# Index tiles in a ring of eight, and a gather queue that waits for products itself

## The chip, the cores and the metric
One core of a Trainium2 chip. The metric is the device time of one launch in microseconds; the kernel before takes 5577.5 us (median of 3 runs, 5574.76 to 5580.09). Lower is better.

## What is computed
One graph layer with 12,500 nodes of 128 features and 412,500 edges, sorted by destination.

```
f      = x @ W1            (node features; a second part, self, stays with the node)
w      = gelu(gelu(edge_attr_8 @ W_mlp1) @ W_mlp2) @ Wp     (radial weights of each edge)
mid    = products of w, f[src] and edge_attr_4              (per edge; scalars and vectors mixed)
n      = segment_sum(mid, dst)                              (over the edges of each node)
out    = layernorm(x + cos * self + sin * (n @ W2))
```

All of it is float32. The order of edges and the indices are data: f[src] is a gather from a table in DRAM.

## The kernel before
**Start.** The node features are computed (PE), copied (DVE) and stored as `feature_table` in DRAM; source indices are transposed to `src_all` (int16, one column for each tile of 128 edges). `acc` holds the 12,500 nodes' sums in SBUF.

**Main loop.** Edges are worked on in 202 blocks of 2048, each 16 tiles of 128 edges, or 4 chunks of 4 tiles. Each engine has its own list of instructions, a loop of 25 rounds of 8 steps (POOL: of 4 steps), and they meet only in semaphores. For block b:

- ACT copies 16 index columns from `src_all` to `idx` as int32 (`copy_indices`, L496) and increments `s_idx`.
- POOL waits for `s_idx`, and issues 16 indirect DMAs (`gather`, L429), each of which brings 128 rows of 512 bytes from the table to `gath`, a ring of 4 slots. They increment `s_g[slot][chunk]` on landing.
- PE makes the radial weights: two layers for block b+4 (L700, L705; their gelus are ACT L512 and L517) and the weights of block b by chunks into four PSUM banks (L715, `s_w[c]`).
- DVE multiplies weights and gathered rows (`products`, L957 and L960, `s_prod[c]`), when `s_w[c]`, `s_g[slot][c]` and `s_seg[c]` of the block before are there.
- PE sums the products into windows of 8 nodes (L729, `s_seg[c]`); ACT copies the sums (L531), PE transposes them (L740), ACT copies that (L538, L539), PE multiplies by W2 (L748, `s_y`), and DVE adds 16 windows to `acc` (L985).
- SP loads edge attributes (L341) and, for two blocks at a time, edge_attr_8 (L337).

The order on each engine is written out by hand in its function `step`. On DVE it is: product chunks 0 and 1, `select` for the next block, chunk 2, loading of 16 window addresses, chunk 3, the additions of block b-1. On PE: radial 0, sums 2 of b-1, first layer, radial 1, sums 3 of b-1, second layer, radial 2, transposes of b-1, sums 0, first layer, radial 3, sums 1, the product with W2 of b-1, second layer, transposes of b.

**What frees a slot.** ACT does it for POOL. At the head of step b, ACT waits until DVE has done chunk 3 of block b-1, and then copies the indices of block b+3, whose slot in `gath` and in `idx` is that of b-1. POOL itself waits for nothing but `s_idx`:

```
act.wait_ge(s_prod[CHUNKS - 1], b + 0)
copy_indices(b + (SLOTS - 1), (s + SLOTS - 1) % SLOTS).then_inc(s_idx, 1)
```

A second branch (`Else`) of every engine is for graphs in which the nodes of a group of edges spread over more than 8; it isn't taken with these inputs. After the loop the nodes are normalised and stored.

Of the kernel before, what the change touches and what calls it, by code (L numbers as in the profile page):

```python
# [43 lines left out]
SLOTS = 4  # L44
# [21 lines left out]
def build_program(nc, x, src, dst, ea4, ea8, W1_0e, W1_1o, W_mlp1, W_mlp2, Wp, W2_0e, W2_1o, out):  # L66
# [3 lines left out]
    with ctx:  # L70
        def sb(name, shape, dt=FP32):
            return ctx.enter_context(nc.sbuf_tensor(name, shape, dt))
# [9 lines left out]
        big = sb("big", [128, NODE_TILES * FEAT])  # L82
        dst_rows = sb("dst_rows", [128, ROWS, 256])
        rel_all = sb("rel_all", [128, ALL_GROUPS * 2], BF16)
        src_all = sb("src_all", [128, (BLOCKS + 2) * TILES], INT16)
        gath = sb("gath", [128, SLOTS, TILES, FEAT])
        idx = sb("idx", [128, SLOTS, TILES], INT32)
        ea_t = sb("ea_t", [128, RING, TILES, 4])
        ea_last = sb("ea_last", [128, TILES, 4])
        e8 = sb("e8", [128, RING, 128])  # L90
# [197 lines left out]
        def _(sp):  # L288
# [71 lines left out]
            with sp.If(flag < WINDOW):  # L360
# [16 lines left out]
                for i in range(PAIRS):  # L377
                    sp.wait_ge(s_tr, 2 * ROUNDS + (i // 2 - 1))
                    for r in range(2 * i, 2 * i + 2):
                        load_e8(r, min((b + r) * BLOCK, LAST_START))  # L380
            with sp.Else():
                with sp.Fori(1, BLOCKS - 1) as b:
                    sp.wait_ge(s_gblk, b + 1)
                    load_e8(0, b * BLOCK)
                    sp.dma_start(ea_t[:, 0, :, :], ea4[bass.ds(b * BLOCK, BLOCK), :].rearrange("(t q) k -> q t k", q=128))\
                        .then_inc(s_ea[0], 16)
                sp.wait_ge(s_gblk, BLOCKS)
                load_e8(0, LAST_START)
# [8 lines left out]
        @block.gpsimd  # L397
        def _(pool):
            pool.memset(wfeat[:, :], 0.0).then_inc(s_zero_node, 1)
            pool.memset(wself_raw[:, :], 0.0).then_inc(s_zero_node, 1)  # L400
            pool.memset(ident[:, :], 0.0).then_inc(s_ident0, 1)
            pool.wait_ge(s_ident0, 1)
            pool.affine_select(out=ident[:, :], in_=ident[:, :], compare_op=ALU.not_equal, fill=1.0, base=0,
                               pattern=[[-1, 128]], channel_multiplier=1).then_inc(s_ident, 1)
            pool.memset(dst_rows[:, ROWS - 1, :], 0.0).then_inc(s_rows, 1)
            pool.iota(iota_i[:, :], pattern=[[1, WINDOW]], base=0, channel_multiplier=0).then_inc(s_iota, 1)
            pool.memset(eps_col[:, :], EPS).then_inc(s_iota, 1)
            pool.memset(w1bd[:, :, :], 0.0).then_inc(s_zero, 1)
            pool.memset(w2bd[:, :], 0.0).then_inc(s_zero, 1)
            pool.memset(wpbd[:, :], 0.0).then_inc(s_zero, 1)  # L410
            pool.memset(conv_stage[:, :, :], 0.0).then_inc(s_zero, 1)
            pool.memset(ea_last[:, :, :], 0.0).then_inc(s_eal0, 1)
            pool.wait_ge(s_zero, 4)
            for to, of in loop_weights[:POOL_WEIGHT_LOADS]:
                pool.dma_start(to, of).then_inc(s_wts_pool, 16)

            for c in range(ROWS):
                pool.wait_ge(s_min, c + 1)
                for e in range(2):
                    half = slice(128 * e, 128 * (e + 1))  # L420
                    last = pool.tensor_scalar(dst_rows[:, c, half], dst_rows.bitcast(INT32)[:, c, half],
                                              base_f[:, ROWS * e + c:ROWS * e + c + 1], None, ALU.subtract)
                last.then_inc(s_rel, 1)
            pool.wait_ge(s_xts, -(-(SRC_FROM + 2 * ROWS) // BATCH))
            pool.memset(src_rows[:, ROWS - 1, :], 0.0).then_inc(s_srcz, 1)

            def gather(s, c):
                for t in range(CT * c, CT * (c + 1)):
                    pool.indirect_dma_start(out=gath[:, s, t, :], out_offset=None, in_=table[:, :],  # L429
                                            in_offset=bass.IndirectOffsetOnAxis(ap=idx[:, s, t:t + 1], axis=0))\  # L430
                        .then_inc(s_g[s][c], 16)

            def table_stored():
                for i in range(PIECE_SLOTS):
                    pool.wait_ge(s_tab[i], 16 * (len(range(i, PIECES, PIECE_SLOTS)) + (i == (PIECES - 1) % PIECE_SLOTS)))

            table_stored()
            pool.wait_ge(s_flag, 1)
            flag = pool.value_load(flag_i[0:1, 0:1], min_val=0, max_val=NODES)
            with pool.If(flag < WINDOW):  # L440
                for b in range(SLOTS):
                    pool.wait_ge(s_idx, b + 1)
                    for c in range(CHUNKS):
                        gather(b, c)
                with pool.Fori(1, QUADS) as n:
                    for s in range(SLOTS):

                        pool.wait_ge(s_idx, n * SLOTS + (s + 1))
                        pool.sem_inc(s_round, 1)
                        for c in range(CHUNKS):  # L450
                            gather(s, c)
                for b in (BLOCKS - 2, BLOCKS - 1):
                    pool.wait_ge(s_idx, b + 1)
                    for c in range(CHUNKS):

                        if b < BLOCKS - 1 or c >= CUT_C:
                            gather(b % SLOTS, c)
            with pool.Else():
                with pool.Fori(0, BLOCKS) as b:
                    pool.wait_ge(s_idx, b + 1)  # L460
                    pool.sem_inc(s_round, 1)
                    for c in range(CHUNKS):
                        gather(0, c)
# [5 lines left out]
        def _(act):  # L469
# [69 lines left out]
                act.copy(to[:, :, 1:4, :], by_tile(1)[:, :, 1:4, :]).then_inc(s_zt, 1)  # L539

            def step(b, s, k, d_round, first=False, last=False):
                if not last and not first:
                    act.wait_ge(s_prod[CHUNKS - 1], b + 0)
                    copy_indices(b + (SLOTS - 1), (s + SLOTS - 1) % SLOTS).then_inc(s_idx, 1)
                if not first:
                    copy_transposed(b - 1, 0)
                if not last:
                    if s % SUPER == 0:
                        copy_e8T(k)
                    gelu1(b + SUPER, 0)  # L550
                if not first:
                    copy_sums(b - 1, 1)
                if not last:
                    gelu2(b + SUPER, s + SUPER, 0)
                    lay_attributes(b + 1, (s + 1) % RING, d_round * 16 + 16, b + 1, None if first else b + 0)
                if not first:
                    copy_transposed(b - 1, 1)
                if not last:
                    gelu1(b + SUPER, 1)
                copy_sums(b, 0)  # L560
                if not last:
                    gelu2(b + SUPER, s + SUPER, 1)
# [2 lines left out]
            flag = act.value_load(flag_i[0:1, 0:1], min_val=0, max_val=NODES)  # L565
            act.wait_ge(s_rts[0], 2)
            with act.If(flag < WINDOW):
                for b in range(SLOTS):
                    copy_indices(b, b).then_inc(s_idx, 1)
                copy_odd_indices()  # L570
                copy_e8T(0)
# [526 lines left out]
```

## Time and profile before

| | |
|---|---|
| device time, median of 3 | 5577.5 us |
| profiled execution: time, span | 5586.11 us, 5584.3 us |
| busy: PE, PE weight loads | 58%, 32% of the span |
| busy: POOL, DVE, ACT | 56%, 34%, 21% |
| DMA engines, mean | 46 GB/s |
| PE's granted clock, mean | 0.74 of 2.4 GHz |

The profile is of one execution. A group of instructions has a source line, an engine, an operation, and what it writes and reads. Busy time of PE comes from modelled ends of its instructions. "Idle before" is the time in which the engine did nothing ahead of an instruction, with the line that ended this; "remote" or "another core or an unknown queue" stands for a semaphore's update that was not matched with the end of an instruction, and "issue" for no wait that the profile shows. Times in the timeline count from the start of the span.

### The profile page before, as it was taken

What the parts mean: (1) busy time and instruction counts of PE and PEld (TensorE: products, weight loads), DVE (VectorE), ACT (ScalarE), POOL (GpSimd) and SP (SyncE); (2) the same over time, 40 slices, a digit from 0 to 9 for tenths busy, and PEclk for the clock granted to TensorE, in tenths of its full rate; (3) what the DMA queues carried; (4) which work ended last, traced back from release to release, by engine and by line L of the source; (5) the groups of instructions that cost most, each with busy time, mean ns of one, the idle gap of its engine ahead of it and who ended that gap; (6) DMA issues with size and microseconds to landing.
All of it is one profiled execution on the core that took longest, in us unless ns stands there. A gap on an engine that the chain in (4) does not pass through costs nothing.

```text
span 5584.3 us, 54049 instructions
## 1 busy us (share of the span) xinstructions
PE 3213.1 (58%) x15272; PEld 1784.0 (32%) x15272; DVE 1871.9 (34%) x6401; ACT 1200.0 (21%) x2642; POOL 3103.5 (56%) x3281
## 2 busy tenths in 40 slices
PE   5655555555555555555555555555555555556556
PEld 4232333333323333333233333332332333333334
DVE  2233333333333333333333333333333333333335
ACT  2121222112212222222122222221221222222224
POOL 5255555555555555555555555555555556555551
PEclk7677777777777777777777777777777777777777
DMA  6022122221221221222212212122122122221211
GB/s 148 16 45 45 42 43 43 44 44 42 44 46 41 44 45 43 43 43 44 45 41 44 45 43 42 43 44 44 41 44 45 42 43 45 44 43 42 45 45 58
DMA packets 586056, 256.02 MB, mean 46 GB/s; under 512 B 528384, under 2 KB 531868, under 8 KB 584348
## 3 DMA queue, kind: packets, MB, share of 16 engines
q0 software_dynamic: 103616, 211.52, 15.0%
q1 hardware_dynamic: 480572, 42.82, 6.6%
q14 instruction: 160, 1.30, 0.1%
q10 hardware_dynamic: 1696, 0.18, 0.0%
q8 instruction: 12, 0.20, 0.0%
HBM read 241.45 MB, written 12.81 MB: 46 GB/s over the span
## 4 chain that ended last, share of the span: by engine, by line
another core or an unknown queue 50%; PE 31%; issue 10%; ACT 8%; DVE 0%; ACTq 0%; DMA 0%; DVEq 0%; SPq 0%; POOL 0%; POOLq 0%
PE bank L715 9%; PE bank L705 7%; PE bank L700 5%; PE bank L729 4%; PE bank L740 4%; ACT h L512 2%; ACT zsb L531 2%; ACT bank L527 1%; PE bank L657 1%; ACT ztsb L539 1%; ACT ztsb L538 1%; PE bank L696 1%; PE bank L748 1%; ACT big L615 1%
## 5 line engine op out<-in xcount | busy, mean ns | idle before, releaser
L429 POOL DMA_INDIRECT gath<-feature_table,idx x3224 | 3077.3, 955 | 2351.9 <-ACT idx L496 1395.0
L705 PE MATMUL bank<-h,w2bd 128*128 128x512 f32 x820 | 631.2, 861 | 897.3 <-ACT h L512 512.2
L957 DVE TENSOR_TENSOR big<-bank,gath 128x256 f32<-128x256 f32 x808 | 341.8, 423 | 2358.2 <-remote 2112.0
L715 PE MATMUL bank<-wpbd,big 128*128 128x256 f32 x3232 | 986.3, 434 | 50.2 <-issue 49.0
L715 PEld LDWEIGHTS bank<-wpbd,big 128*128 128x128 f32 x3232 | 700.0, 224 | 443.1 <-issue 377.9
L960 DVE TENSOR_TENSOR big<-bank,gath 128x384 f32<-128x384 f32 x1616 | 818.0, 548 | 0.0
L985 DVE TENSOR_TENSOR acc<-acc,bank 128x8 f32 x3232 | 528.5, 164 | 777.5 <-remote 361.2
L748 PE MATMUL bank<-ztsb,conv 128*128 128x128 f32 x1616 | 316.0, 356 | 681.8 <-issue 549.2
L740 PE MATMUL bank<-ident,zsb 128*128 128x128 f32 x1616 | 337.3, 347 | 559.4 <-ACT zsb L531 491.4
L512 ACT ACTIVATE h<-bank 128x512 f32<-128x512 f32 x410 | 244.9, 597 | 1748.9 <-remote 1182.8
L729 PE MATMUL bank<-big,sel 128*32 128x256 f32 x6464 | 560.7, 421 | 9.4 <-DVE big L960 6.8
L700 PE MATMUL bank<-e8T,w1bd 128*128 128x512 f32 x820 | 506.6, 702 | 56.2 <-ACT big L517 38.7
L517 ACT ACTIVATE big<-bank 128x512 f32<-128x512 f32 x410 | 453.2, 1105 | 388.5 <-PE bank L705 254.8
L740 PEld LDWEIGHTS bank<-ident,zsb 128*128 128x128 f32 x1616 | 257.3, 180 | 840.1 <-ACT zsb L531 626.4
L748 PEld LDWEIGHTS bank<-ztsb,conv 128*128 128x128 f32 x1616 | 268.2, 251 | 773.5 <-issue 647.4
L705 PEld LDWEIGHTS bank<-h,w2bd 128*128 128x128 f32 x820 | 158.6, 241 | 1035.9 <-ACT h L512 553.0
L531 ACT COPY zsb<-bank 128x512 f32<-128x512 f32 x404 | 236.1, 584 | 926.0 <-remote 736.5
L538 ACT COPY ztsb<-bank 128x64 f32<-128x64 f32 x404 | 86.9, 215 | 1032.6 <-remote 843.9
L700 PEld LDWEIGHTS bank<-e8T,w1bd 128*128 128x128 f32 x820 | 136.1, 209 | 276.2 <-issue 173.1
L729 PEld LDWEIGHTS bank<-big,sel 128*32 128x32 f32 x6464 | 133.0, 112 | 274.0 <-issue 273.8
L944 DVE TENSOR_TENSOR sel<-rel_all,bank 128x128 f32<-128x128 f32 (+1 forms) x202 | 58.0, 287 | 421.9 <-issue 269.8
L949 DVE TENSOR_TENSOR sel<-sel,bank 128x512 f32<-128x512 f32 x202 | 138.7, 687 | 6.9
(77 smaller groups left out, 794.3 us busy)
## 6 DMA issues: line engine op xcount, KB each, us to landing
gath<-feature_table,idx POOLq DMA_INDIRECT x3224
e<-in_edge_attr SPq DMA_DIRECT2D x416, 32.0 KB
ea_t<-in_edge_attr SPq DMA_DIRECT2D x100, 64.0 KB
feature_table<-gath SPq DMA_DIRECT2D x4, 1280.0 KB, 5.6
out<-big SPq DMA_DIRECT2D x4, 1280.0 KB
big<-in_x SPq DMA_DIRECT2D x3, 1280.0 KB, 8.4
dst_rows<-in_dst SPq DMA_DIRECT2D x1, 1536.0 KB
big<-in_src SPq DMA_DIRECT2D x1, 1408.0 KB
```

The costliest lines, as they stand in the source:

```text
L429: pool.indirect_dma_start(out=gath[:, s, t, :], out_offset=None, in_=table[:, :], in_offset=bass.IndirectOffsetOnAxis(ap=idx[:, s, t:t + 1 ...
L512: act.activation(h1[:, h, :], hid_ps[:, :], ACT.Gelu_apprx_tanh, scale=1.0 / math.sqrt(RADIAL)).then_inc(s_h1[h], 1)
L517: act.activation(h2[:, m // SUPER % 2, :, :, 2 * (m % SUPER) + h], hid_ps[:, :].rearrange("q (b p) -> q b p", b=SUPER), ACT.Gelu_apprx_tan ...
L531: act.copy(zsb[:, :, :], z_ps).then_inc(s_zc, 1)
L700: pe.matmul(hid_ps[:, :], w1bd[:, 2 * (m % SUPER) + h, :], e8T[:, :], start=True, stop=True)\
L705: pe.matmul(hid_ps[:, :], w2bd[:, :], h1[:, h, :], start=True, stop=True).then_inc(s_h2p[h], 1)
L715: last = pe.matmul(wgt_ps[c][:, 256 * r:256 * (r + 1)], h2[:, s // SUPER % 2, s % SUPER, 16 * g:16 * (g + 1), :].rearrange("q p a -> q (p ...
L729: last = pe.matmul(z_ps[32 * t:32 * (t + 1), c % 2, :], sel[:, s % 2, CT * c + t, :, :].rearrange("q k w -> q (k w)"), prod[:, c, t, :], s ...
L740: last = pe.transpose(zt_ps[:, h, c, :], zsb[:, c, 128 * h:128 * (h + 1)], ident[:, :])
L748: last = pe.matmul(y_ps, conv[:, k, :], ztsb[:, k, :], start=(k == 0), stop=(k == 3))
L960: last = dve.tensor_tensor(o[:, :, h, 1:4, :], w[:, :, h, 1, :].unsqueeze(2).to_broadcast([128, n, 3, MUL]), f[:, :, 1:4, :], ALU.mult)
L985: dve.tensor_tensor(acc[:, at], acc[:, at], y_ps[:, WINDOW * t:WINDOW * (t + 1)], ALU.add)\
```

## The change
`idx` becomes a ring of 8 tiles. ACT copies the indices of block b+7 instead of b+3, in the middle of step b instead of at its head, and eight blocks instead of four before the loop. POOL waits for `s_idx` as before, and now also, ahead of each chunk of four gathers, for `s_prod[c]` of the block four back; its loop has 25 rounds of 8 blocks instead of 50 of 4. `s_round` is incremented once for each chunk instead of once for each block. The waits in SP's `Else` are in the branch that isn't taken.

```diff
-        src_all = sb("src_all", [128, (BLOCKS + 2) * TILES], INT16)
+        src_all = sb("src_all", [128, (BLOCKS + RING - 2) * TILES], INT16)
...
-        idx = sb("idx", [128, SLOTS, TILES], INT32)
+        idx = sb("idx", [128, RING, TILES], INT32)
...
             with sp.Else():
+                for i in range(1, PAIRS):
+                    sp.wait_ge(s_e8[i], 64)
+                    sp.wait_ge(s_ea[i], 16)
...
             def gather(s, c):
                 for t in range(CT * c, CT * (c + 1)):
-                    pool.indirect_dma_start(out=gath[:, s, t, :], ...
+                    pool.indirect_dma_start(out=gath[:, s % SLOTS, t, :], ...
...
-                        .then_inc(s_g[s][c], 16)
+                        .then_inc(s_g[s % SLOTS][c], 16)
...
-                for b in range(SLOTS):
+                def gather_block(b, s, free, chunks=range(CHUNKS)):
                     pool.wait_ge(s_idx, b + 1)
-                    for c in range(CHUNKS):
-                        gather(b, c)
-                with pool.Fori(1, QUADS) as n:
-                    for s in range(SLOTS):
-
-                        pool.wait_ge(s_idx, n * SLOTS + (s + 1))
-                        pool.sem_inc(s_round, 1)
-                        for c in range(CHUNKS):
-                            gather(s, c)
+                    for c in chunks:
+                        if free is not None:
+                            pool.wait_ge(s_prod[c], free)
+                            pool.sem_inc(s_round, 1)
+                        gather(s, c)
+
+                for b in range(RING):
+                    gather_block(b, b, b - SLOTS + 1 if b >= SLOTS else None)
+                with pool.Fori(1, ROUNDS) as n:
+                    for s in range(RING):
+                        gather_block(n * RING + s, s, n * RING + (s - SLOTS + 1))
+                gather_block(BLOCKS - 2, 0, BLOCKS - 2 - SLOTS + 1)
+                gather_block(BLOCKS - 1, 1, BLOCKS - 1 - SLOTS + 1, range(CUT_C, CHUNKS))
...
             def step(b, s, k, d_round, first=False, last=False):
-                if not last and not first:
-                    act.wait_ge(s_prod[CHUNKS - 1], b + 0)
-                    copy_indices(b + (SLOTS - 1), (s + SLOTS - 1) % SLOTS).then_inc(s_idx, 1)
...
                 if not first:
                     copy_sums(b - 1, 1)
+                if not last and not first:
+                    act.wait_ge(s_prod[CHUNKS - 1], b + 0)
+                    copy_indices(b + (RING - 1), (s + RING - 1) % RING).then_inc(s_idx, 1)
...
-                for b in range(SLOTS):
+                for b in range(RING):
                     copy_indices(b, b).then_inc(s_idx, 1)
```

## Rows read from the trace of the kernel before

**Rows 1.** The page's chain of work that ended last, by engine.
```profile
another core or an unknown queue 50%; PE 31%; issue 10%; ACT 8%; DVE 0%; ACTq 0%; DMA 0%; DVEq 0%; SPq 0%; POOL 0%; POOLq 0%
```
**Rows 2.** Waits: line, released by, us in total, times, longest us.
```profile
POOL gath L429 <- ACT idx L496: 1395.0, 197, 97.3
...
DVE big L957 <- remote: 2112.0, 266, 15.0
...
ACT h L512 <- remote: 1182.8, 182, 15.0
```
**Rows 3.** The tile idx: duration ns min/median/max, first and last start.
```profile
L429 POOL DMA_INDIRECT gath<-feature_table,idx x3224: 949/955/1071, 70.8 to 5484.6; - x190
L496 ACT CAST idx<-src_all x204: 198/231/245, 68.2 to 5502.3; 128x16 int32 x100, 128x16 int32<-128x16 int16 x2
```
**Rows 4.** Timeline 2055 to 2081: start, duration, what, [idle before <-releaser].
```profile
2055.86 0.95 POOL L429 DMA_INDIRECT gath<-feature_table,idx  x1 [8.09 <-ACT idx L496]
...
2060.19 0.58 ACT L531 COPY zsb<-bank 128x512 f32<-128x512 f32 x1 [0.86 <-PE bank L729]
...
2062.98 1.12 PE L700 MATMUL bank<-e8T,w1bd 128*128 128x512 f32 x2
...
2063.94 1.03 PE L715 MATMUL bank<-wpbd,big 128*128 128x256 f32 x4
...
2074.22 0.60 ACT L512 ACTIVATE h<-bank 128x512 f32<-128x512 f32 x1 [8.06 <-remote]
...
2074.74 0.95 POOL L429 DMA_INDIRECT gath<-feature_table,idx  x1 [0.30 <-issue]
...
2077.05 0.42 DVE L957 TENSOR_TENSOR big<-bank,gath 128x256 f32<-128x256 f32 x1 [12.19 <-remote]
2077.39 1.01 DVE L960 TENSOR_TENSOR big<-bank,gath 128x384 f32<-128x384 f32 x2
...
2078.71 4.59 DVE L985 TENSOR_TENSOR acc<-acc,bank 128x8 f32 x16 [0.31 <-remote]
...
2079.89 0.24 ACT L496 CAST idx<-src_all 128x16 int32 x1
...
2080.92 0.95 POOL L429 DMA_INDIRECT gath<-feature_table,idx  x1 [5.22 <-ACT idx L496]
```
**Rows 5.** Timeline 2038 to 2055, the block before.
```profile
2038.52 1.03 PE L715 MATMUL bank<-wpbd,big 128*128 128x256 f32 x4
...
2039.20 9.74 SPq L337 DMA_DIRECT2D e<-in_edge_attr  x4
...
2046.82 0.95 POOL L429 DMA_INDIRECT gath<-feature_table,idx  x1 [0.30 <-issue]
...
2051.20 0.60 ACT L512 ACTIVATE h<-bank 128x512 f32<-128x512 f32 x1 [4.12 <-remote]
2051.26 0.43 DVE L957 TENSOR_TENSOR big<-bank,gath 128x256 f32<-128x256 f32 x1 [11.22 <-remote]
...
2051.69 0.58 ACT L531 COPY zsb<-bank 128x512 f32<-128x512 f32 x1
...
2054.84 0.23 ACT L496 CAST idx<-src_all 128x16 int32 x1
```
**Rows 6.** Timeline 5490 to 5503, behind the last gather.
```profile
5490.54 0.23 ACT L496 CAST idx<-src_all 128x16 int32 x1
...
5502.26 0.22 ACT L496 CAST idx<-src_all 128x16 int32 x1
```
**Rows 7.** Groups of the page: busy us, mean ns of one, idle before.
```profile
L729 PE MATMUL bank<-big,sel 128*32 128x256 f32 x6464 | 560.7, 421 | 9.4 <-DVE big L960 6.8 <-issue 2.6
L985 DVE TENSOR_TENSOR acc<-acc,bank 128x8 f32 x3232 | 528.5, 164 | 777.5 <-remote 361.2 <-DVE acc L985 16.4 <-PE bank L748 9.2
```
**Rows 8.** Windows 248 to 5512: us, busy (x instructions) of PE, PEld, DVE, ACT, POOL, clock, DMA, GB/s.
```profile
248.00:5512.00 5264.00, 3029.38 (x14575) 1664.33 (x14574) 1765.92 (x5981) 1103.82 (x2446) 3015.95 (x3160) 0.74 0.21 43
```

More of the change, by code:

```diff
@@ L428, in gather @@
                 for t in range(CT * c, CT * (c + 1)):
-                    pool.indirect_dma_start(out=gath[:, s, t, :], out_offset=None, in_=table[:, :],
+                    pool.indirect_dma_start(out=gath[:, s % SLOTS, t, :], out_offset=None, in_=table[:, :],
                                             in_offset=bass.IndirectOffsetOnAxis(ap=idx[:, s, t:t + 1], axis=0))\
-                        .then_inc(s_g[s][c], 16)
+                        .then_inc(s_g[s % SLOTS][c], 16)
             def table_stored():
@@ L440, in _ @@
             with pool.If(flag < WINDOW):
-                for b in range(SLOTS):
+                def gather_block(b, s, free, chunks=range(CHUNKS)):
                     pool.wait_ge(s_idx, b + 1)
-                    for c in range(CHUNKS):
-                        gather(b, c)
-                with pool.Fori(1, QUADS) as n:
-                    for s in range(SLOTS):
-                        pool.wait_ge(s_idx, n * SLOTS + (s + 1))
-                        pool.sem_inc(s_round, 1)
-                        for c in range(CHUNKS):
-                            gather(s, c)
[L452 to L457, printed above, removed]
+                    for c in chunks:
[10 more added lines that the diff above has]
+                gather_block(BLOCKS - 1, 1, BLOCKS - 1 - SLOTS + 1, range(CUT_C, CHUNKS))
             with pool.Else():
```

## The prediction
> **What bounds the kernel now.** I read the chain of waits first: half of the span is put down to "another core or an unknown queue" [rows 1]. With one core there is no other, so this is a release whose source the profile does not match. The waits name it: DVE's product L957 waits 2112.0 us for "remote" and ACT's L512 1182.8 us, while POOL waits for ACT's index copy 197 times [rows 2]. Without the longest wait (97.3 us, the start) that is (1395.0 - 97.3) / 196 = 6.62 us for each block.
>
> Then the timeline. POOL's 16 gathers of a block start 1.26 us apart, from 2055.86 to 2074.74, and end at 2075.69: a run of 19.83 us, 5.03 us for each chunk of four. The next run starts at 2080.92, right behind the index copy at 2079.89 [rows 4]. Run plus mean pause: 19.83 + 6.62 = 26.45 us a block. All the rest of a step, when no gather is under way, takes far less: the last two index copies, after the last gather (5484.6 [rows 3]), are 5502.26 - 5490.54 = 11.7 us apart [rows 6]. So neither PE's work (3029.38 us busy in 5264 us, 15.2 us a block [rows 8]) nor POOL's alone sets 26.45 us; something ties them.
>
> Rows 4 show what. PE's first-layer matmul starts at 2062.98 and its radial matmuls at 2063.94, but their consumers start at 2074.22 (ACT L512, 8.06 us "remote") and 2077.05 (DVE L957, 12.19 us "remote"). Early in the same run nothing is late: at 2060.19 ACT follows PE by its own 0.86 us. So some 5.5 us into a run of gathers PE's results begin to reach the others late. Between ACT L512 and DVE L957 lie four recorded matmuls: 2.83 / 4 = 0.71 us each, however small. When the run ends, everything comes at once [rows 5]: POOL's last gather ends at 2047.77 and ACT L512, DVE L957 and ACT L531 start at 2051.20, 2051.26 and 2051.69, on results of three different PE groups. I call this the release: 2078.71 - 2075.69 = 3.0 us behind the end of a run, 3.5 us in rows 5, where SP's e8 loads (L337, 9.74 us) lie in the run.
>
> The loop is therefore a circle: gathers run, PE's results stall, gathers end, release, ACT finishes the step, ACT copies indices, gathers run. Each block holds one run and one pause.
>
> The Trainium skill (Perfetto Trace Analysis, Summary: the profiler window per engine type) says that a TensorE record's end is only estimated, and what follows it is hidden. By it PE could really be executing that slowly; the common release in rows 5 speaks for late delivery, and the forecast is the same by both, since it uses only when consumers start.
>
> **The change, part by part.**
> *Index ring of eight, seven ahead.* In a step the index copy moves from the head to behind copy_sums. It stays one copy of 0.24 us [rows 4] on ACT, so a step's total keeps it; where it stands now it can delay gelu2 by 0.24 us, where it stood it delayed the transposed copy as much. I take 0. Four more copies in the prologue are 4 x 0.24 = 1 us at most, hidden by POOL's 97.3 us wait. The waits in SP's other branch are not executed. What the move does is to take ACT, and PE's last layer behind which ACT stands, out of POOL's circle: the copy for a block is done seven steps before.
>
> *POOL's waits.* Each chunk now waits for products(b-4, c). POOL may run up to four blocks ahead instead of starting block b+3 at step b. Could it run on for ever? No: a block has 14575 / (5264 / 26.45) = 73 recorded matmuls [rows 8], and at 0.71 us each PE would pass 52 us a block while POOL gathers one in 20. So POOL runs out of free chunks, pauses, and the release follows. What changes is what a pause consists of and how often it comes. Behind the waiting instruction stand only POOL's own gathers. They are needed four blocks later, so nobody else waits for them.
>
> *Length of a pause.* Before: release, rest of the step on ACT (gelu, last layer, gelu), index copy, POOL's start: 6.62 us in the mean; 8.1 us between rows 5 and rows 4 (in front of 2055.86) and 5.2 us at the end of rows 4. After: release (3.0 us without, 3.5 us with e8 loads), the product that frees the chunk (2077.05 to 2078.40, 1.35 us), POOL's start (index copy's end 2080.13 to gather 2080.92, 0.8 us): 5.15 to 5.65 us, mean 5.4.
>
> *How often.* A run now ends where the products are four blocks back, not after 16 gathers. From a release, PE goes on undisturbed through the pause and about 5.5 us of the next run: 2.2 + 5.5 = 7.7 us of an 11.7 us step. Then 12 us and more of the run at 0.71 us a matmul pass some 20 of 73, and at the next release what PE has done meanwhile comes at once (rows 5: the layer, the radial chunk, the sums: 8 records for a chunk's sums alone [rows 7], some 20). That is 0.66 + 0.27 + 0.27 = 1.2 blocks for each run, or 4.8 chunks. I take 4.5 chunks, half way between this and the present 4, since the e8 loads slow half of the runs: 4 / 4.5 = 0.9 pauses a block.
>
> *A pause on chunk 0.* If POOL stops in front of chunk 0, the product it needs stands behind DVE's 16 window additions (4.59 us from 2078.71; 164 ns each [rows 7]), which themselves wait for the release: 3.0 + 4.6 + 1.35 + 0.8 = 9.8 us. I take one pause in eight as such: 0.9 x (9.8 - 5.4) / 8 = 0.5 us a block.
>
> *Cost of the added waits.* Four waits with a register and four increments a block where there was one. No row shows a satisfied wait between two chunks. Lower bound 0: they lie under the 0.95 us of the gather before. Upper bound: each costs POOL's 0.8 us start anew, 3 more = 2.4 us. I take 0.3 us, near the lower, because address arithmetic between chunks is already hidden there (all starts 1.26 us apart).
>
> *Sum.* Pause time a block: 0.9 x 5.4 + 0.5 + 0.3 = 5.7 us against 6.62: 0.9 us less. Over 196 blocks: 176 us. The profiled execution took 5586.11 us (span 5584.3), 8.6 us over the median of the three runs: 5586 - 176 = 5410, less 9: 5400 us.
> Ends: 5 chunks a run, short release, no cost of waits: 0.8 x 5.15 = 4.1 us, so 2.5 x 196 = 490 us less, 5087. Waits at their upper bound: 2.1 x 196 = 412 us more than the forecast, 5810.
>
> **Rivals.**
> *A, POOL stops at chunk 0 (slower).* If the weights of chunk 3 become visible before POOL has done its four chunks, POOL takes that chunk too and stops in front of chunk 0, where the pause is 9.8 us. With five chunks a run: 0.8 x 9.8 + 0.3 = 8.1 us a block, 1.5 us more than now, 297 us: 5875 us. It decides at 15 to 17 us after a run's start. For it: a chunk-0 stop leaves DVE and PE far advanced, so it may repeat itself. Against it: in rows 4 chunk 3's weights come at 2077.05, 21 us after the run's start, and in rows 5 only with the release.
> *B, nothing gained.* One pause a block remains, and the 1.2 us that it gets shorter are lost to slower results, since each run begins earlier in PE's step and more of the step falls into it: 26.45 us a block, 5577 us.
> *C, gathers free of interference (much faster).* If what delays PE's results is the burst after a wait and not gathering itself, steps take 11.7 us and POOL's 20.1 us a block bounds: 5577 - 6.3 x 196 = 4340 us. The Trainium skill (SBUF — State Buffer, SBUF: two separate sides) says that DMA ports and engine ports cannot contend and that PE never waits for anyone's port; by that rule PE should be as fast beside gathers as without, and the time would be rival C's. The trace does not agree: 12.19 us late beside them [rows 4], 11.7 us for a whole step without [rows 6].
>
> **How the numbers follow.** Forecast 0.58, rival A 0.24, B 0.12, C 0.06. A change under 0.2% (11 us) is not told from none. Faster: 0.58 + 0.06 and a quarter of B: 0.67. Same: half of B, 0.06. Slower: 0.24 and the rest of B: 0.27. The forecast's own range is 5087 to 5570. The range goes from 5060 to 5830: it leaves out C and the worse half of A.
>
> **What would show it.** POOL L429 then waits for DVE L960, not for ACT L496. Right: pauses of 5 to 6 us, fewer than one a block, POOL's idle time before L429 down by some 180 us; DVE L957 still "remote". Wrong: most pauses near 10 us in front of chunk 0, behind L985 (A); more than one pause a block, or gathers more than 1.26 us apart at chunk borders (the waits' price); "remote" gone (C). If DVE waited for a gather itself, the claim that gathers are early enough would be wrong.

## The result, and the profile after

The changed kernel takes 5652.75 us (median of 4 runs, 5633.84 to 5687.63) against 5578.8 us for the kernel before on the same chip (4 runs, 5574.76 to 5584.6). The ratio is 1.0139 (95% interval 1.0087 to 1.019): 1.4% slower. The forecast was 5400 us, so the direction was wrong; the range of 5060 to 5830 holds the time. On other chips, reached by the experiments, the same change makes the kernel 0.24% faster; that comes last among them.

The profiled execution took 5646.39 us with a span of 5644.4 us, 60.1 us more than before. First the page: two groups and the shares of the chain of waits.

```profile
L432 POOL DMA_INDIRECT gath<-feature_table,idx x3224 | 3077.2, 954 | 2407.5 <-issue 1719.1
...
L986 DVE TENSOR_TENSOR acc<-acc,bank 128x8 f32 x3232 | 528.1, 163 | 1574.9 <-remote 1137.2
...
another core or an unknown queue 44%; PE 32%; issue 15%; ACT 6%; DVE 2%; DVEq 0%; DMA 0%; ACTq 0%; SPq 0%; POOL 0%; POOLq 0%
```

The 3224 gathers are as busy as before, and the idle time ahead of them is 2407.5 us, where it was 2351.9 us: 55.6 of the 60.1 us stand there. The line of the window additions (now L986) waits 1137.2 us for late results, where it was 361.2 us [rows 7]. The waits name who releases POOL, and what DVE and ACT wait for (line, released by, us in total, times, longest).

```profile
POOL gath L432 <- issue: 1719.1, 3033, 83.2
...
DVE big L958 <- remote: 1287.9, 194, 14.9
DVE acc L986 <- remote: 1137.2, 145, 18.3
...
ACT h L513 <- remote: 745.6, 94, 20.0
...
POOL gath L432 <- DVE big L961: 688.4, 191, 10.4
```

ACT's index copy no longer releases POOL; DVE's product L961 does, as predicted. The view names it for 112 of the 213 pauses counted below and says "issue" for the other 101 (a good part of the semaphores' updates isn't in this trace, see under Open); but in 212 of the 213 POOL starts 0.77 to 0.79 us after the end of an L961. "Remote" has not gone. It has moved: 2112.0 us at the products and 1182.8 us at ACT's first gelu before [rows 2], now spread over the products, the additions and ACT. The usual 0.30 us between gathers (the median) stayed at chunk borders too, so a satisfied wait costs nothing to see.

I then went through all gathers of the trace from block 5 on and took every gap over 1.2 us as a pause:

| kernel | pauses | mean us | sum us | chunks per run | where |
|---|---|---|---|---|---|
| before | 197 | 6.60 | 1300.9 | 4.0 | chunk 0 always |
| after | 213 | 6.41 | 1364.4 | 3.7 | chunk 0: 162, mean 6.87; chunk 1: 27, 5.10; chunk 2: 4, 8.21; chunk 3: 19, 4.21; one within a chunk |

Pauses cost 63.5 us more, the start 14 us less (the pause ahead of block 4, 97.25 before, is 83.22 us), and the other gaps 6 us more: 55.6 us.

Three pauses in four are in front of chunk 0. One of the long ones in full, from the timeline (start, duration, what, idle before):

```profile
1872.24 0.95 POOL L432 DMA_INDIRECT gath<-feature_table,idx  x1 [0.30 <-issue]
1875.22 0.58 ACT L532 COPY zsb<-bank 128x512 f32<-128x512 f32 x1 [11.58 <-remote]
...
1876.04 1.10 ACT L518 ACTIVATE big<-bank 128x512 f32<-128x512 f32 x1 [0.23 <-remote]
1876.10 4.59 DVE L986 TENSOR_TENSOR acc<-acc,bank 128x8 f32 x16 [8.61 <-remote]
...
1880.66 0.42 DVE L958 TENSOR_TENSOR big<-bank,gath 128x256 f32<-128x256 f32 x1
1881.00 1.01 DVE L961 TENSOR_TENSOR big<-bank,gath 128x384 f32<-128x384 f32 x2
...
1882.80 0.95 POOL L432 DMA_INDIRECT gath<-feature_table,idx  x1 [9.60 <-DVE big L961]
```

The run's last gather ends at 1873.19. DVE's additions begin 2.91 us later, on the release; the product of chunk 0 can only follow them at 1880.66, ends at 1882.01, and POOL starts 0.79 us after. 2.9 + 4.6 + 1.35 + 0.8 = 9.6 us: this is rival A's pause, term for term.

Not every pause on chunk 0 is like it. Two blocks earlier the additions fell into the run itself:

```profile
1817.44 4.61 DVE L986 TENSOR_TENSOR acc<-acc,bank 128x8 f32 x16 [4.16 <-remote]
...
1822.62 0.95 POOL L432 DMA_INDIRECT gath<-feature_table,idx  x1 [0.30 <-issue]
1825.82 0.42 DVE L958 TENSOR_TENSOR big<-bank,gath 128x256 f32<-128x256 f32 x1 [3.78 <-remote]
...
1826.16 1.01 DVE L961 TENSOR_TENSOR big<-bank,gath 128x384 f32<-128x384 f32 x2
...
1827.94 0.95 POOL L432 DMA_INDIRECT gath<-feature_table,idx  x1 [4.36 <-issue]
```

I sorted the 213 pauses by whether all 16 additions stand between the run's end and the product that ends the pause. 64 hold them: 10.14 us in the mean, 648.9 us in sum, all on chunk 0. The other 149 have a mean of 4.80 us, 715.5 us in sum.

### The profile page after: what moved, and what is told of

It reads as the page before. It is cut to its first block, busy times and chain, and to the rows that moved or that the text cites. A ratio compares the mean times of both kernels' runs of the same rounds, so it can differ in the third digit from the quotient of the medians.

```text
span 5644.4 us, 54565 instructions
## 1 busy us (share of the span) xinstructions
PE 3152.4 (56%) x15272; PEld 1726.7 (31%) x15272; DVE 1866.7 (33%) x6401; ACT 1227.9 (22%) x2646; POOL 3103.4 (55%) x3281
## 3 DMA queue, kind: packets, MB, share of 16 engines
q0 software_dynamic: 103616, 211.52, 14.4%
## 4 chain that ended last, share of the span: by engine, by line
another core or an unknown queue 44%; PE 32%; issue 15%; ACT 6%; DVE 2%; DVEq 0%; DMA 0%; ACTq 0%; SPq 0%; POOL 0%; POOLq 0%
PE bank L716 9%; PE bank L701 7%; PE bank L706 5%; PE bank L730 5%; PE bank L741 2%; ACT h L513 2%; ACT zsb L532 1%; ACT big L518 1%; PE bank L749 1%; PE bank L658 1%; DVE acc L986 1%; ACT ztsb L540 1%; DVE big L961 1%; ACT big L616 1%
## 5 line engine op out<-in xcount | busy, mean ns | idle before, releaser
L432 POOL DMA_INDIRECT gath<-feature_table,idx x3224 | 3077.2, 954 | 2407.5 <-issue 1719.1
L716 PE MATMUL bank<-wpbd,big 128*128 128x256 f32 x3232 | 1063.2, 462 | 250.9 <-issue 249.7
L986 DVE TENSOR_TENSOR acc<-acc,bank 128x8 f32 x3232 | 528.1, 163 | 1574.9 <-remote 1137.2
L716 PEld LDWEIGHTS bank<-wpbd,big 128*128 128x128 f32 x3232 | 751.5, 239 | 731.3 <-issue 654.9
L701 PE MATMUL bank<-e8T,w1bd 128*128 128x512 f32 x820 | 585.3, 803 | 662.7 <-ACT big L518 258.7
L706 PE MATMUL bank<-h,w2bd 128*128 128x512 f32 x820 | 524.6, 726 | 691.1 <-ACT h L513 396.3
L961 DVE TENSOR_TENSOR big<-bank,gath 128x384 f32<-128x384 f32 x1616 | 816.6, 546 | 0.0
L741 PE MATMUL bank<-ident,zsb 128*128 128x128 f32 x1616 | 301.5, 318 | 737.9 <-issue 402.4
L730 PE MATMUL bank<-big,sel 128*32 128x256 f32 x6464 | 587.8, 440 | 23.0 <-DVE big L961 22.8
L741 PEld LDWEIGHTS bank<-ident,zsb 128*128 128x128 f32 x1616 | 229.9, 164 | 918.1 <-issue 525.6
L706 PEld LDWEIGHTS bank<-h,w2bd 128*128 128x128 f32 x820 | 143.4, 219 | 818.3 <-ACT h L513 437.3
L749 PE MATMUL bank<-ztsb,conv 128*128 128x128 f32 x1616 | 235.4, 289 | 9.9 <-issue 9.9
L749 PEld LDWEIGHTS bank<-ztsb,conv 128*128 128x128 f32 x1616 | 196.9, 192 | 93.4 <-issue 93.4
```

The costliest lines, as they stand in the source:

```text
L432: pool.indirect_dma_start(out=gath[:, s % SLOTS, t, :], out_offset=None, in_=table[:, :], in_offset=bass.IndirectOffsetOnAxis(ap=idx[:, s, ...
L701: pe.matmul(hid_ps[:, :], w1bd[:, 2 * (m % SUPER) + h, :], e8T[:, :], start=True, stop=True)\
L706: pe.matmul(hid_ps[:, :], w2bd[:, :], h1[:, h, :], start=True, stop=True).then_inc(s_h2p[h], 1)
L716: last = pe.matmul(wgt_ps[c][:, 256 * r:256 * (r + 1)], h2[:, s // SUPER % 2, s % SUPER, 16 * g:16 * (g + 1), :].rearrange("q p a -> q (p ...
L730: last = pe.matmul(z_ps[32 * t:32 * (t + 1), c % 2, :], sel[:, s % 2, CT * c + t, :, :].rearrange("q k w -> q (k w)"), prod[:, c, t, :], s ...
L741: last = pe.transpose(zt_ps[:, h, c, :], zsb[:, c, 128 * h:128 * (h + 1)], ident[:, :])
```

## The experiments

Each is told against the kernel before on its own chip, since that takes 5677.96 us on the chip of e1 to e4 (5667.03 to 5687.19), 5583.56 on that of e5 to e8 (5581.25 to 5594.34), and 4216 to 4217 on the three of e9 to e18. Pauses are counted as above. All edits are to the changed kernel unless said otherwise.

### e1: one wait a block, for chunk 3

```diff
+                    if free is not None:
+                        pool.wait_ge(s_prod[CHUNKS - 1], free)
+                        pool.sem_inc(s_round, 1)
                     for c in chunks:
-                        if free is not None:
-                            pool.wait_ge(s_prod[c], free)
-                            pool.sem_inc(s_round, 1)
                         gather(s, c)
```

> The changed kernel with one wait of POOL a block in place of four: before the first gather of a block it waits for products chunk 3 of the block four back. Theory (the time is 20.1 us of gathers plus a pause whose length is set by the product that POOL waits for): every pause ends behind chunk 3, 3.0 to 3.5 us release + 1.35 us product + 0.8 us start = 5.2 to 5.6 us, 25.5 us a block, about 5400 us; pauses on chunk 0 behind DVE's additions are gone. Rival 1 (PE's late results are a budget of so much a block, wherever the pause lies): one pause of 6.6 us or more a block remains, 5580 to 5650 us. Rival 2 (the four waits and increments a block are what the change costs): 5590 us, as before.

5597.82 us is the median of four runs (5517.66, 5596.82, 5598.83 and the profiled 5611.24 us). The ratio, 0.9814 (0.9739 to 0.9888), is of the three others, and leans on the 5517.66; by the medians it is 0.986. The time is within rival 1's 5580 to 5650 us and above the theory's 5400. The edit asks for the same product as the kernel before does through ACT, so it is the change without its chunk waits: ACT's late end of the step is out of POOL's way. It gains between 1.1 and 2.6% on this chip, but its 197 pauses are not what I had priced: 6.71 us in the mean (1321.8 us in sum), where my term was 5.4. (No trace shows the kernel before on this chip; on the first its pauses were 6.60 us.) A pause of its timeline says why:

```profile
1904.73 0.95 POOL L432 DMA_INDIRECT gath<-feature_table,idx  x1 [0.30 <-issue]
...
1908.66 0.42 DVE L958 TENSOR_TENSOR big<-bank,gath 128x256 f32<-128x256 f32 x1 [1.90 <-remote]
...
1909.00 1.01 DVE L961 TENSOR_TENSOR big<-bank,gath 128x384 f32<-128x384 f32 x2
...
1910.00 0.42 DVE L958 TENSOR_TENSOR big<-bank,gath 128x256 f32<-128x256 f32 x1
...
1910.35 1.01 DVE L961 TENSOR_TENSOR big<-bank,gath 128x384 f32<-128x384 f32 x2
...
1911.42 4.60 DVE L986 TENSOR_TENSOR acc<-acc,bank 128x8 f32 x16
...
1912.13 0.95 POOL L432 DMA_INDIRECT gath<-feature_table,idx  x1 [6.44 <-issue]
```

At the release (1908.66, 3.0 us behind the run's end at 1905.68) DVE has two chunks' products before it, not one: 3.0 + 2 x 1.35 + 0.8 = 6.5 us. So it is in 138 of its 197 pauses; 51 hold one chunk's product. I read this as a run that begins earlier in the step and leaves more of the step to the next release.

### e2: one wait a block, for chunk 0

```diff
+                    if free is not None:
+                        pool.wait_ge(s_prod[0], free + 1)
+                        pool.sem_inc(s_round, 1)
```
The chunk waits are taken out as in e1. All pauses now lie in front of chunk 0, whose product stands behind the additions in DVE's order.

> The same with the wait for products chunk 0 of the block three back, so that every pause ends behind chunk 0 and thus behind the 16 additions. Theory: release 3.0 + additions 4.6 + product 1.35 + start 0.8 = 9.8 us each, at most 29.9 us a block, 6250 us; but PE and DVE are further on when gathers start again, so some releases come before a run's end: 6.9 us, the mean of the changed kernel's pauses on chunk 0, is the lower end, 5650 us. Rival 1 (a budget of late results): the same time as with chunk 3. Rival 2 (cost of waits): faster than the changed kernel by the same as with chunk 3.

6002.12 us (5969.63 to 6015.14), ratio 1.0554 (1.0514 to 1.0594). It lies in the range that was written down, 5650 to 6250 us. 172 pauses of 9.89 us in the mean, some 4.6 chunks to a run. That the mean meets the 9.8 us worked out for a pause on chunk 0 is luck: sorted as above, 104 pauses hold the additions, with a mean of 13.05 us, and 68 don't, with 5.07. It is the slowest kernel of all. Its idle time ahead of the gathers:

```profile
L432 POOL DMA_INDIRECT gath<-feature_table,idx x3224 | 3085.8, 957 | 2762.6 <-issue 2356.7 <-DVE big L961 405.9
```

### e3: the additions moved behind chunk 0 of the next block

In DVE's step, chunk 0 of the next block is multiplied first, and then the additions are made. (The last block gathers all four chunks, 8 gathers more.)

```diff
-                for c in range(CHUNKS):
+                for c in range(1, CHUNKS):
...
+                if not last:
+                    products(b + 1, s + 1, 0, round_ + ((s + 1) % SLOTS == 0))
```

> The changed kernel with DVE's 16 additions of block b-1 moved behind product chunk 0 of block b+1 (POOL's waits as in the change; the last block's first two chunks are gathered too, 10 us of POOL beside other work). Theory: the pauses on chunk 0 lose the 4.6 us of additions; with 157 pauses of 6.85 us there, of which those over 6 us stand behind additions, some 2 to 4 us a block less: 4900 to 5250 us. Rival 1 (budget): within 1% of 5650 us. Rival 2: 5650 us too, since the waits stay.

5476.24 us (5457.23 to 5500.91), ratio 0.9636 (0.961 to 0.9661): 3.6% under the kernel before on that chip. Less than I wrote down (4900 to 5250), but the direction is clear. Pauses on chunk 0 fall to 131 with a mean of 4.70 us; in all there are 240, 3.3 chunks to a run, and their sum is 1148.3 us. One of them:

```profile
1799.60 0.42 DVE L958 TENSOR_TENSOR big<-bank,gath 128x256 f32<-128x256 f32 x1 [11.09 <-remote]
1799.94 1.01 DVE L961 TENSOR_TENSOR big<-bank,gath 128x384 f32<-128x384 f32 x2
...
1800.87 2.81 DVE L986 TENSOR_TENSOR acc<-acc,bank 128x8 f32 x10
...
1801.75 0.95 POOL L432 DMA_INDIRECT gath<-feature_table,idx  x1 [4.71 <-DVE big L961]
```

The product is now first at the release and POOL starts 2.15 us after it. None of the 240 pauses holds the additions in front of its product. Together with the sorting of the changed kernel's pauses (10.14 us with the additions, 4.80 without) and of e2's (13.05 and 5.07) this shows the additions as what makes the long pauses long.

### e4: a quarter of the gathers

`gather` issues one tile of a chunk's four from block 4 on, and the products wait for 16 increments each; the other rows are not fetched.

> The changed kernel with one gather for each chunk instead of four from block 4 on (three of four tiles of gathered rows are stale; it leaves out three quarters of the gathers). Theory (gathers delay PE's results, and what PE has queued comes when they end): POOL's part is 5 us a block, PE's results are hardly ever late, a step takes 12 to 18 us, 2700 to 3900 us. Rival (PE with its throttled clock and the chain over three engines need some 25 us a block anyway): 5300 to 5600 us.

2788.46 us, ratio 0.4912 (0.4901 to 0.4923), within the theory's range, and a view of the main loop by its window (columns as in [rows 8]):

```profile
248.00:2700.00 2452.00, 2366.55 (x14496) 1345.65 (x14493) 1747.24 (x5951) 1112.77 (x2433) 752.13 (x786) 1.00 0.20 29
```

PE is busy 97% of this window at a granted clock of 1.00, the upper level of 2.4 GHz, where it was 58% at 0.74 [rows 8]. So the rival, a throttled PE that needs some 25 us a block anyway, is out. No "remote" of any size is left (79.3 us is the largest, in the preparations). Late results need the dense gathers; whether by their number or by their bytes this run can't tell, since it cuts both. A block takes (2700 - 248) / 196 = some 13 us.

### e5: 24 more matmuls a block (on the kernel before)

```diff
-                pe.matmul(hid_ps[:, :], w1bd[:, 2 * (m % SUPER) + h, :], e8T[:, :], start=True, stop=True)\
+                for q in range(4):
+                    last = pe.matmul(hid_ps[:, 128 * q:128 * (q + 1)], w1bd[:, 2 * (m % SUPER) + h, :],
...
```

The matmuls of both layers, cut from 512 columns into four of 128.

> The kernel before with each of the four 128x512 layer matmuls of a block cut into four of 128x128: the same columns, 24 more recorded matmuls a block (97 for 73). Theory (while gathers run, PE's results pass one recorded matmul in 0.71 us, however small): of the 24 some two thirds fall into the late part of a run, 16 x 0.71 = up to 11 us a block, less what the release takes at once: 2 to 8 us a block, 5950 to 7100 us. Rival (PE computes slowly beside gathers, by columns): the time of the kernel before within 2%.

5823.95 us, ratio 1.0426 (1.0405 to 1.0447); pauses 197 as before, mean 7.76 instead of 6.60. Neither expectation holds: 24 more matmuls added (5823.95 - 5583.56) / 196 = 1.2 us a block, below the 2 to 8 us and above the rival's 2%. This does not refute a fixed time for each late matmul. A run is 16 gathers long in both kernels, so by that account it passes as many late matmuls in both, and what is left over is done after the release. PE's busy time alone grew by about 1 us a block (3029.38 us in 5264 us before, 3187.59 us in 5442 us here). The times of PE's own semaphore updates say more. Where two in a row are late, the time from one to the next over four recorded radial matmuls is 2.86 us (median of 55 pairs) before and 2.85 us (135 pairs) here, again 0.71 us for each; over the eight recorded matmuls of a cut second layer it is 3.59 us (53 pairs), 0.45 us for each. All these scatter widely, and what the rate goes by stays open.

### e6, e7, e8: the same edits on another chip

e6 is e1 and e3 together. e7 is the changed kernel once more. e8 is the kernel before with e3's move of the additions only.

> One wait a block for chunk 3 together with the additions moved behind the next chunk 0. Theory: with one wait on chunk 3 no pause stands behind the additions, so the move brings nothing more than it did alone at chunk 3: ratio 0.97 to 0.985, and no better than the moved additions with four waits (0.964). Rival (the moved additions also let PE's product with W2 and so the rest of a step come earlier): the two gains add up, ratio 0.945 to 0.955.

> The changed kernel itself on the chip of the other runs, for a comparison on one chip. Expected the same ratio to the kernel before as at first, 1.01 to 1.02.

> The kernel before, with nothing changed but the additions of block b-1 moved behind chunk 0 of block b+1 (and the last block's first two chunks gathered too). Theory (the additions count only where a pause of POOL ends behind them; before, it ends behind ACT's index copy): within 1% of the kernel before. Rival (the additions are on the step's path whatever POOL waits for): 3% faster or more, as in the changed kernel.

| | us | ratio to before | pauses | mean us | sum us |
|---|---|---|---|---|---|
| e6 | 5629.32 | 1.009 (1.0062 to 1.0119) | 196 | 6.73 | 1318.5 |
| e7 | 5674.63 | 1.0165 (1.0144 to 1.0186) | 220 | 6.28 | 1382.4 |
| e8 | 5763.87 | 1.0318 (1.0294 to 1.0343) | 197 | 7.48 | 1472.8 |

e7 repeats the result: 162 pauses on chunk 0, mean 6.86, as in the first trace. e6 is 0.9% slower than before on this chip, although both of its parts were faster on theirs; neither its theory (0.97 to 0.985) nor its rival met it. Its pauses are e1's (6.71), and not e3's (4.78): behind one wait for chunk 3 the place of the additions doesn't matter to POOL. It is 0.8% faster than e7, the changed kernel on the same chip (5629.32 to 5674.63 us). e8's expectation, within 1% of before, was wrong: moving the additions is no gain in itself. PE's product with W2 then waits longer for ACT's copy of the transposed sums, in the groups of the kernel before and of e8:

```profile
L748 PE MATMUL bank<-ztsb,conv 128*128 128x128 f32 x1616 | 316.0, 356 | 681.8 <-issue 549.2 <-ACT ztsb L539 132.4
...
L746 PE MATMUL bank<-ztsb,conv 128*128 128x128 f32 x1616 | 325.0, 363 | 948.2 <-ACT ztsb L537 581.6 <-issue 364.4 <-DVE sel L947 2.2
```

The idle time ahead of it grew by 266 us, and it lies in the part of the step whose end ACT's index copy stands behind. That this is what makes e8 slower is my reading; no run tests it. e3's gain isn't that of the move alone: neither with ACT's release (e8) nor with one wait a block (e6) do the pauses get shorter, only with the chunk waits, whose pauses on chunk 0 it cuts.

### e9 to e12: the bytes, and the candidates once more

e9 is the changed kernel with gathers of 32 elements a row instead of 128 from block 4 on (128 instead of 512 bytes; the rest of a row is not fetched, and as the indices stay as they are, the pieces all come from the first quarter of the table). e10 repeats e1, e11 e3, e12 the changed kernel.

> The changed kernel with gathers of 32 elements (128 bytes) a row instead of 128 (512 bytes) from block 4 on: as many gathers and rows, a quarter of the bytes (the products then use rows of which three quarters are stale). If the bytes that the gathers move are what delays PE's results: much nearer to the quarter gathers' 2788 us, 3000 to 4500 us. If it is the number of gathers or of their rows: within 3% of the changed kernel, some 5500 to 5700 us.

> One wait a block, chunk 3 four back, on one chip with the changed kernel. Theory: 1 to 3% faster than the changed kernel (its pauses are 6.7 us, 193 of them, against 6.85 us on chunk 0 plus some 50 shorter ones). Against the kernel before 0.98 to 1.00, since on the chip of the first comparison the kernel before itself took 5678 us and not 5580.

> The changed kernel with the additions moved behind the next chunk 0, once more on one chip with the changed kernel. Theory: 3 to 5% faster than the changed kernel; against the kernel before 0.96 to 0.985.

> The changed kernel on this chip, for the comparison with the two above: 1.01 to 1.02 of the kernel before if that ratio is the same on every chip; 0.99 to 1.00 if the kernel before is slower on this chip and the changed one is not.

The chip of these runs was another. The kernel before takes 4216.99 us there (32 runs, 4215.0 to 4218.5), 24% less than on the first, and the expectations had been made for late results.

| | us | ratio to before |
|---|---|---|
| e9 | 4206.79 | 0.9977 (0.9967 to 0.9988) |
| e10 | 4216.59 | 0.9999 (0.999 to 1.0008) |
| e11 | 4215.88 | 0.9998 (0.9989 to 1.0007) |
| e12 | 4206.57 | 0.9976 (0.9966 to 0.9985) |

The changed kernel's waits on this chip, with the chain of its page:

```profile
DVE big L958 <- DMA gath<-feature_table,idx: 1113.2, 384, 3.9
PE bank L730 <- DVE big L961: 1075.5, 507, 6.5
...
POOL 68%; issue 23%; PE 6%; ACT 1%; DVE 1%; DMA 1%; POOLq 1%; ACTq 0%; DVEq 0%; SPq 0%
```

"Remote" is gone, DVE waits for gathers, and POOL never pauses behind its first wait for a slot: its gaps are 0.30 us, and the longest is 0.60. A block takes 16 x 1.26 = 20.2 us, which is rival C's world (forecast as 4340 us). ACT starts right behind PE in the middle of a run of gathers, in a fourth run of the changed kernel (e16, below):

```profile
2002.05 1.13 PE L701 MATMUL bank<-e8T,w1bd 128*128 128x512 f32 x2
...
2003.21 0.60 ACT L513 ACTIVATE h<-bank 128x512 f32<-128x512 f32 x1 [2.52 <-PE bank L701]
```

PE ends at 2003.18 by the record, ACT starts 0.03 us later; before, the same pair was 10.1 us apart [rows 4]. The number of bytes makes no difference here (e9 beside e12), because POOL takes 955 ns for a gather of either width. Whether fewer bytes would make results less late where they are late stays open.

### e13 to e18: the same, again

e13 to e16 repeat the four on one more chip, e17 and e18 repeat e3 and the changed kernel on another. Both are of the kind without late results (before: 4216.29 and 4216.8 us).

> The changed kernel with rows of 128 bytes from block 4 on (three quarters of each gathered row are stale). Where the kernel before takes some 5600 us: if the bytes of the gathers are what delays PE's results, 4200 to 4900 us; if it is the number of gathers or their rows, within 3% of the changed kernel. Where it takes 4217 us, nothing is told apart: 4207 us again.

> One wait a block for chunk 3. Where the kernel before takes some 5600 us (PE's results late): 1 to 3% faster than the changed kernel on the same chip. Where it takes 4217 us: the same as all.

> The additions behind the next chunk 0, with four waits. Where the kernel before takes some 5600 us: 3 to 5% faster than the changed kernel on the same chip, since the pauses on chunk 0 lose the additions. Rival (the gain of 3.6% at first came from that chip, where the kernel before took 5678 us): no faster than the changed kernel. Where it takes 4217 us: the same as all.

> The changed kernel on the same chip. Where the kernel before takes some 5600 us: 1.01 to 1.02 of it. Where it takes 4217 us: 0.998 of it, since POOL's gathers alone set the time of both.

> The additions behind the next chunk 0, with four waits. Where the kernel before takes some 5600 us: 3 to 5% faster than the changed kernel on the same chip. Rival: no faster than it. Where the kernel before takes 4217 us: the same as all.

> The changed kernel beside it. Where the kernel before takes some 5600 us: 1.01 to 1.02 of it. Where it takes 4217 us: 0.998 of it.

4206.67 (0.9978), 4215.65 (1.0), 4215.11 (0.9998), 4206.46 (0.9976), 4215.1 (0.9995) and 4206.63 us (0.9975), each with an interval of about 0.001 to both sides and as written down for chips of this kind. They settle where the 0.24% comes from. POOL's first wait for a slot, ahead of block 4, in e14 (one wait a block) and then in e16 (the changed kernel):

```profile
168.80 0.96 POOL L432 DMA_INDIRECT gath<-feature_table,idx  x1 [17.70 <-issue]
```
```profile
158.96 0.95 POOL L432 DMA_INDIRECT gath<-feature_table,idx  x1 [8.03 <-issue]
```

By chunks it waits 8.03 us once, by blocks 17.70: the 9.7 us are the whole difference between 4215.65 and 4206.46. e15 starts as early (8.59 us) and gives it back with its 8 more gathers, 8 x 1.26 = 10.1 us. The 14 us that the changed kernel gains at its start on the first chip are the same saving: with late results the pause ahead of block 4 is 83 to 86 us in the four traces with chunk waits (the changed kernel twice, e3, e4) and 94 to 99 us in the six others.

## Why the prediction was wrong

**The circle: right.** Gathers run, results come late, the release follows 2.9 to 3.0 us behind a run's end in the pauses shown, POOL's idle time holds the loss. e4 and e9 to e18 show both sides: without dense gathers, and on chips without late results, nothing of it is left.

**Ring and index copy: right.** ACT's copy is out of POOL's waits, and no row shows a cost of it.

**Cost of the added waits: taken as 0.3 us a block, measured 0.** The median gap is 0.305 us at a chunk border and within a chunk.

**Length of an ordinary pause: right, and somewhat long.** 5.4 us counted the release, one chunk's product and POOL's start. The 149 pauses without the additions have a mean of 4.80 us, since many releases come less than 3.0 us after a run's end (2.25 us in the short one shown). (In e1, with one wait for chunk 3, most pauses hold two products and the mean is 6.71 us; that is rival B's mechanism, but it isn't what the changed kernel does: there 211 of 213 pauses hold one.)

**A pause on chunk 0: the step that failed.** I took one pause in eight as standing behind the additions, 22 of 176. Measured: 162 of 213 pauses are on chunk 0, and 64 of them, three in ten of all, hold the 16 additions. Their price was right (9.8 us forecast, 10.14 us measured). In the sum from block 5 on: forecast 154 x 5.4 + 22 x 9.8 = some 1050 us and 59 us for the waits; measured 715.5 + 648.9 = 1364 us. So the ordinary pauses gave 116 us less than forecast and the waits 59 us less, and the pauses behind the additions cost 433 us more. That is the whole miss.

**How often: also off.** I took 4.5 chunks a run (176 pauses); it is 3.7 (213 pauses). The ordinary pauses number 149 against 154, so the surplus is again the pauses behind the additions.

The two hang together. A run that starts on chunk 0 goes on for four chunks; chunks 1 to 3 are free and chunk 0 isn't, since DVE stands ahead of the additions or in them. 107 of the 207 runs that start between 300 and 5450 us are of exactly 16 gathers. I had called this rival A and gave it 0.24; its place and its mechanism are what happened, and its 5875 us was too high because it put the additions into every pause. Against it I had put that chunk 3's weights come late in a run. That spoke about runs of the kernel before, which begin at another point of the step, and so decided nothing. That the range of 5060 to 5830 us holds the time owes something to luck: its upper end was made of 2.1 us a block for waits that cost nothing.

**A reading of rows 4 that was loose.** The 0.86 us that the prediction gives as ACT's distance behind PE is ACT's idle time ahead of that copy; PE's L729 ended 0.07 us before it. Nothing in the sum uses it.

**What holds in place of "fewer pauses".** In five traces with late results the time lost in pauses hardly depends on how POOL's runs are cut. e1, e6, the changed kernel twice and the kernel before lie between 1301 and 1382 us with 196 to 220 pauses. I read this as PE and DVE needing a certain quiet time for each block, which runs of gathers don't give; moving the stop trades number for length. e2, with the additions in 104 of 172 pauses (1701.9), and e3, with none in the way (1148.3), break out. So do e8 (1472.8) and e5 (1528.5), both with ACT's release as before. That this quiet time is a fixed need was not tested by itself.

**Open.** What makes results late in some runs and not in others. The first comparison and e1 to e8 had them, e9 to e18, on three other chips, did not; but each chip that is named on record was used at one time only, and all the late runs came before all the others, so that chip and time aren't told apart. It isn't that the gathers' own packets take longer: 14.4% of the span is 813 us in the changed kernel on the first chip, and 19.3% is 811 us in e12.

```profile
q0 software_dynamic: 103616, 211.52, 14.4%
...
q0 software_dynamic: 103616, 211.52, 19.3%
```

One thing goes with the lateness in the traces: semaphore updates are missing from the record. In the trace of the kernel before 9664 of the gathers' 51584 landing updates are there, in e12 51078; of the updates by PE, ACT and DVE 8274 of 10031, in e12 10002 of 10035. And e4, with hardly any late result, on a chip that has them, still lacks half (6997 of 13664 landings). The kernels' waits are met all the same, so the record, not the semaphores, loses them. Every run here has a granted clock on record, so it isn't excluded that the recording itself takes part.

What a late result's rate goes by (e5). How much of e3's 3.6% is its chip's: e3 and the changed kernel never ran on one chip with late results, and on e3's chip the kernel before was itself 1.8% slower than on the first. e1 (0.9814) and e6 (1.009), with the same pauses, stand to their own kernels before 2.8% apart. In plain times e3's 5476 us is under every other kernel's with late results (the changed kernel: 5653 and 5675). It is the version to take further: faster than the kernel before on the one chip with late results where it ran, level with it on those without, where its 8 extra gathers could be cut.

## What to carry to other kernels

Here POOL was stopped by results that its own gathers delay. In such a circle a wait that lets it start earlier gives no time back by itself: count how much of the consumers' step is left at each stop. Before a wait is moved from "the whole block" to "this chunk", look at what stands ahead of each chunk's producer in its engine's order, since the stop will come to lie on the dearest of them. Price such a stop by how often the dear work really stands in it: one in eight was a guess, and the guess was the miss. And a comparison made on one chip can have the other sign on the next: run the kernel before beside each.

## What the runs showed of the hardware that was not expected

- The same kernel takes 5578.8, 5677.96 and 5583.56 us in the first comparison, e1 to e4 and e5 to e8, and 4216.99, 4216.29 and 4216.8 us on the three chips of e9 to e18, each within 0.4% in its own runs. For the changed kernel the idle time ahead of the same 3224 gathers is 2407.5 us on the first and 1005.1 us in e12, 1402 of the 1440 us between the two profiled executions (5646.39 and 4206.01).
- By the Trainium skill (SBUF — State Buffer, SBUF: two separate sides) engines don't wait for DMA ports. e16 agrees, since PE's results come 0.03 us behind their record beside gathers; the trace of the changed kernel on the first chip does not, where ACT waited up to 20.0 us for them. No run here says what differs, nor that ports are what does it.
- In the pauses shown, late results come some 3.0 us after the last gather (2.9 in the changed kernel, 3.0 in e1, 3.0 and 3.5 before [rows 4, 5]). In the changed kernel's 64 long pauses the additions start 2.94 us after it in the median, and in one in ten 1.4 us or less.
- A gather of 128 rows holds POOL for 955 ns and 1.26 us from start to start, for rows of 512 and of 128 bytes alike (e12, e9).
- PE's mean granted clock in the main loop, between its two levels of 1.2 and 2.4 GHz, was 0.74 for the kernel before with late results [rows 8], 0.88 for the changed kernel on the chip without, and 1.00 in e4. The higher clock went with the absence of late waits. In e4 only the gathers and the waits for them were changed, so there the rise of the clock came of that edit and not the other way round.
